# Moving the statistics of x1's third chunk from VectorE to ScalarE in a fused mix, group-norm and convolution-scan kernel

## The reference

```python
x = x + mix(_gn(x), centers, spreads, token_bias)      # a 128x128 map over the positions, one for each of 4 heads
x = x + scan(_gn(x), W)                                # carry = row + relu(conv1d(carry, W)), row after row

def _gn(v, G=32, eps=1e-05):
    g = v.reshape(B_, H_, W_, G, C_ // G)
    m = jnp.mean(g, axis=(1, 2, 4), keepdims=True)
    s = jnp.var(g, axis=(1, 2, 4), keepdims=True)
    return ((g - m) / jnp.sqrt(s + eps)).reshape(v.shape)
```

## Time and profile before

| | before |
|---|---|
| median of three runs | 765.4 us (765.18 to 765.99) |
| profiled execution: its own time | 766.88 us |
| profiled execution: span | 765.1 us |
| PE busy | 681.2 us (89%) |
| DVE busy | 595.5 us (78%) |
| ACT busy | 490.2 us (64%) |
| POOL busy | 429.6 us (56%) |
| granted TensorE clock, mean | 0.973 |

### The profile page before, as it was taken

How to read it: one execution, slowest core, us unless ns; L and a number is a source line. 1 busy time by engine, 2 the same in 40 slices (tenths; PEclk the granted TensorE clock), 3 DMA queues, 4 the chain that set the end, 5 groups by cost and what they waited for, 6 DMA issues and landing times.

```text
span 765.1 us, 18263 instructions
## 1 busy us (share of the span) xinstructions
PE 681.2 (89%) x5100; PEld 648.2 (85%) x5100; DVE 595.5 (78%) x1426; ACT 490.2 (64%) x854; POOL 429.6 (56%) x416
## 2 busy tenths in 40 slices
PE   1578777776999999999899999996999999999995
PEld 1466666666999999999799999986999999999995
DVE  7578999983898888896979898774667677767774
ACT  1156777776676777766676768746666666666661
POOL 1555555661666766665576767752655555555554
PEclk9888999997999999999999999997999999999998
DMA  9855565322355555554555543331444444444444
GB/s 185 160 111 111 117 132 118 75 63 49 71 106 107 103 100 97 106 102 82 101 108 103 108 82 56 56 53 25 78 71 72 76 72 69 72 75 73 69 75 77
DMA packets 412050, 68.18 MB, mean 89 GB/s; under 512 B 411988, under 2 KB 411988, under 8 KB 411988
## 3 DMA queue, kind: packets, MB, share of 16 engines
q1 hardware_dynamic: 359764, 61.17, 43.8%
q10 hardware_dynamic: 52224, 6.30, 5.3%
HBM read 33.85 MB, written 33.55 MB: 88 GB/s over the span
## 4 chain that ended last, share of the span: by engine, by line
PE 45%; DVE 18%; issue 14%; SPq 8%; ACTq 7%; ACT 6%; DMA 1%; POOL 1%; DVEq 0%; POOLq 0%
PE ps_conv L994 21%; PE ps_conv L998 10%; PE ps_mix L918 8%; SPq L299 7%; ACTq L503 6%; DVE st L605 5%; PE ps_in L931 4%; DVE carry L791 3%; ACT carry_h L513 2%; DVE st L706 2%; DVE x_sb L699 2%; ACT x_paired L469 2%; ACT rows L491 2%; PE ps_small L908 2%; DVE carry_l L801 1%
## 5 line engine op out<-in xcount | busy, mean ns | idle before, releaser
L388 POOL TENSOR_TENSOR total<-x_paired,carry 128x256 f32<-128x256 f32 x256 | 250.1, 977 | 226.7 <-DVE staged L778 220.1
L513 ACT ACTIVATE carry_h<-carry 128x256 fp32r<-128x256 f32 x252 | 105.3, 418 | 176.0 <-DVE carry L791 127.6
L491 ACT ACTIVATE rows<-x_paired,shift,rstd 128x256 f32 (+1 forms) x256 | 213.5, 843 | 0.2
L994 PE MATMUL ps_conv<-carry_h,wh 128*128 128x256 f32 x1280 | 205.8, 291 | 6.2 <-ACT carry_h L513 5.7
L998 PE MATMUL ps_conv<-carry_l,wh 128*128 128x256 f32 x1280 | 194.4, 282 | 1.1 <-DVE carry_l L801 1.1
L994 PE MATMUL ps_conv<-carry_h,wl 128*128 128x256 f32 x1280 | 194.8, 283 | 0.0
L469 ACT ACTIVATE x_paired<-ps_in,shift 64x512 f32<-64x512 f32 (+1 forms) x256 | 175.0, 684 | 30.7 <-PE ps_in L931 26.6
L801 DVE TENSOR_TENSOR carry_l<-carry,carry_h 128x256 fp32r<-128x256 f32 x252 | 138.1, 548 | 55.9 <-ACT carry_h L513 40.0
L994 PEld LDWEIGHTS ps_conv<-carry_h,wh 128*128 128x128 f32 x1280 | 172.1, 191 | 11.2 <-ACT carry_h L513 9.1
L998 PEld LDWEIGHTS ps_conv<-carry_l,wh 128*128 128x128 f32 x1280 | 170.9, 190 | 1.5 <-DVE carry_l L801 1.3
L994 PEld LDWEIGHTS ps_conv<-carry_h,wl 128*128 128x128 f32 x1280 | 172.0, 190 | 0.0
(11 more groups left out here) (89 smaller groups left out, 290.5 us busy)
## 6 DMA issues: line engine op xcount, KB each, us to landing
x_sb<-in_x_dram SPq DMA_DIRECT2D x52, 512.0 KB, 4.1
out_dram<-staged SPq DMA_DIRECT2D x832, 32.0 KB, 1.6
rows<-in_x_dram SPq DMA_DIRECT2D x12, 512.0 KB, 4.0
out_dram<-staged ACTq DMA_DIRECT2D x192, 32.0 KB, 1.8
x_paired<-in_L_conv_W_dram SPq DMA_DIRECT2D x2, 80.0 KB, 2.7
x_paired<-in_L_conv_W_dram SPq DMA_DIRECT2D x2, 64.0 KB, 2.6
x_paired<-v_attention_centers_dram SPq DMA_DIRECT2D x1, 0.0 KB
x_paired<-v_attention_spreads_dram SPq DMA_DIRECT2D x1, 0.0 KB
```

The source lines that it names most:

```text
L388: nc.gpsimd.tensor_tensor(total[s][:, :].rearrange("p (w j) -> p w j", w=WS), x1_rows(wave, it, i, 1, s * WS, WS)[:, 0, :, :], carry[s][:, ...
L491: nc.scalar.activation(rows[:, g % 2, :, w // WS, :, w % WS], x1_rows(wave, it, g * RG, RG, w, 1)[:, :, 0, :], ACT.Identity, scale=rstd2[: ...
L513: nc.scalar.activation(carry_h[s][:, EDGE:EDGE + J, :].rearrange("p j w -> p (j w)"), carry[s][:, :], ACT.Copy).then_inc(high_ready[s], 1)
L994: nc.tensor.matmul(ps_conv[:, s * BANK:s * BANK + SW], w[:, d, :], carry_h[s][:, d:d + J, :].rearrange("p j w -> p (j w)"), start=(w is wh ...
```

## The change

ACT takes over the statistics of the third chunk (number 2) of batches 0 to 6. While it keeps this chunk, each of its four ACTIVATEs also sums what it writes (`accum_out`) into `sums2`. After it has kept chunk 3 of the same batch, and ahead of `dev2_of` of the next, a new function `squares2` runs on ACT: a Copy of 128 x 2 scales the sums to means, then two ACTIVATEs of 128 x 512 square the difference of x1 and the mean and sum it; their element output goes to `staged`, which nothing reads in this stage. Means and sums of squares are written into `st2` in the form that `bn_stats` gives, and the counts there are filled in once at the start. On DVE the two `bn_stats` of this chunk go, for the seven batches, and `moments2` waits for the squares (`squares2_done`) and combines seven results where it combined eight. The keeping of chunk 2 of the next batch waits until the squares have read the sums. Batch 7 and the other stages are as before.

```diff
@@ setup
+        sums2 = sb("sums2", [P, 2])
+        mean_c_ready = sem("mean_c_ready")
+        squares2_done = sem("squares2_done")
@@ ScalarE
-            def keep_in(b, k, wave, bw, c, first, count, free):
+            def keep_in(b, k, wave, bw, c, first, count, free, sums=None):
...
                     ins = nc.scalar.activation(dst[q * C:(q + 1) * C, r:CR:2, :], src[:, q, :, :],
-                                               ACT.Identity, bias=shift1[r * C:(r + 1) * C, k:k + 1])
+                                               ACT.Identity, bias=shift1[r * C:(r + 1) * C, k:k + 1],
+                                               accum_out=None if sums is None else sums[q * C:(q + 1) * C, r:r + 1])
...
+            def squares2(b):
+
+                slot = (TU - 1) * (b % 2)
+                act.wait_ge(in_kept, b * CH + CH - 1)
+                if b > 1:
+                    act.wait_ge(mv_ready, b - 1)
+                nc.scalar.activation(st2[:, slot, 1:6:3], sums2[:, :], ACT.Copy,
+                                     scale=1.0 / (HR * J)).then_inc(mean_c_ready, 1)
+                act.wait_ge(mean_c_ready, b + 1)
+                for r in range(2):
+                    nc.scalar.activation(staged[:, r, :], x1_chunk(0, b, CH - 2)[:, r:CR:2, :],
+                                         ACT.Square, scale=-1.0, bias=st2[:, slot, 1 + 3 * r:2 + 3 * r],
+                                         accum_out=st2[:, slot, 2 + 3 * r:3 + 3 * r]).then_inc(squares2_done, 1)
@@ ScalarE, first stage
                     keep_in(b - 1, (b - 1) % 2, 0, b - 1, CH - 1, 0, 4, None)
+                    squares2(b - 1)
                 dev2_of(b + 1)
...
-                keep_in(b, b % 2, 0, b, 2, 0, 4, None)
+                if b > 0:
+                    act.wait_ge(squares2_done, 2 * b)
+                keep_in(b, b % 2, 0, b, 2, 0, 4, None, sums2 if b < W - 1 else None)
@@ VectorE
+            nc.vector.memset(st2[:, 0:TU:TU - 1, 0:6:3], HR * J)
...
+            def shares(b):
+
+                return isinstance(b, int) and b < W - 1
+
             def stats2(b, wave, bw, c, u):
...
-                nc.vector.bn_stats(st2[:, 2 * c + u, :], x1_unit(wave, bw, c, u)).then_inc(stats2_done, 1)
+                slot = 2 * c + u
+                if shares(b):
+                    slot = 2 * min(c, CH - 2) + u + 1
+                nc.vector.bn_stats(st2[:, slot, :], x1_unit(wave, bw, c, u)).then_inc(stats2_done, 1)

             def moments2(b):
-                seen = held(dve, TU * b + TU)
+                first, last = 0, TU
+                seen = held(dve, TU * b + TU - 2 * (W - 1))
+                if shares(b):
+                    seen = (TU - 2) * (b + 1)
+                    first, last = b % 2, TU - 1 + b % 2
                 alone(dve, consts)
+                if shares(b):
+                    dve.wait_ge(squares2_done, 2 * (b + 1))
                 dve.wait_ge(stats2_done, seen)
-                nc.vector.bn_aggr(mv[:, :], st2[:, :, :].rearrange("p n k -> p (n k)")).then_inc(mv_ready, 1)
+                nc.vector.bn_aggr(mv[:, :], st2[:, first:last, :].rearrange("p n k -> p (n k)")).then_inc(mv_ready, 1)
@@ VectorE, alone_chunk, c == 0
                     stats1(nb, ne, 9, 4)
-                    if b > 0:
-                        stats2(b - 1, 0, b - 1, 2, 0)
-                        stats2(b - 1, 0, b - 1, 2, 1)
                     stats1(nb, ne, 13, 3)
```

## The result

The changed kernel takes 768.2 us as the median of 11 runs (765.84 to 771.04), where the kernel before takes 764.6 beside it (11 runs, 762.92 to 767.38). The ratio is 1.0055, with a 95% interval of 1.0031 to 1.0078: **4.2 us slower**, 2.4 to 6.0 (the two medians are 3.6 apart). The forecast was 766.2 us and "within 0.2%"; the measured time lies in the range, but it moved clearly, and the likeliest case was the wrong one. The profiled execution of the changed kernel took 770.53 us (span 768.7).

What follows compares the result with a forecast made beforehand. ACT's chain of keeps and gaps was taken as the bound, DVE setting only the gap before the next batch's chunk 0. -1.26 - 0.5 + 2.4 + 0.2 = +0.84 us gave a median of 766.2 us, range 763.0 to 768.8.

Steps and rivals of the forecast that it cites:

- the likeliest case: Whole kernel: a time within 0.2% of the kernel before, given a chance of 0.42.
- The saving in the early batches: ACT's gaps before chunk 0 after batches 0 and 1 shrink by 0.69 and 0.32 us; earlier clock gives -0.5.
- The sums while keeping: ACT's four summing keeps of chunk 2 cost 0.48 us a chunk: +2.4 in batches 2 to 6, +0.2 in 0 and 1.
- What bounds the kernel: First stage: DVE sets only ACT's gap from chunk 3 to next chunk 0; its relief brings at most 0.65 us a batch.
- rival 3: First stage: DVE is the bound in earnest, its 9.0 us come back in full, 756.4 us; chance 0.04.
- The parts on DVE: DVE drops 1.28 us a batch, `dev_of` stops being late; `moments2` waits nothing for squares, with over 1 us cover.
- `squares2` in the fourth gap: ACT's gap from chunk 3 to next chunk 0, with Copy and two 0.71 us squares: 1.93 us against 1.98.
- the three terms: Batches 0 and 1: shorter ACT gaps (0.69 and 0.32 saved), early clock -0.5, sums while keeping +0.2 us.
- Rival 2: ACT's sums in chunk 2: accumulator reads not hidden, 0.79 us longer a batch, 768.1 us; chance 0.20.
- its decision point: Unhidden reads on ACT: from 0.62 us a chunk on, the time is over 1.5 us longer.
- Rival 1: ACT's sums in chunk 2: accumulator reads fully overlapped, chunk costs 0.05 us more, 763.9 us; chance 0.30.
- rival 4: ACT's squares: their reads not hidden either, 7 x 0.42 = 2.9 us on top of unhidden keep reads, 771.0 us; chance 0.04.

Runs made afterwards that it cites:

- e12: The kernel before, unedited, run again for its profile alone: 763.35 us, first stage 134.01 us.
- e10: The kernel before, unedited, run again for its profile alone: 765.15 us, first stage 136.34 us.
- e4: Against the kernel before, DVE's two `bn_stats` of chunk 2 left out for seven batches, nothing done on ACT instead: 760.9 us, ratio 0.9930.
- e11: The changed kernel, unedited, run again for its profile alone: 768.95 us, first stage 138.80 us.
- e2: The changed kernel without the sums in ACT's four keeps of chunk 2; Copy, squares and DVE's relief stay: 764.7 us, ratio 0.9987 to the kernel before.
- e7: The changed kernel with only the two keeps summing whose source and destination are the same 64 partitions: 768.2 us in one run, period 17.18 us.
- e8: The changed kernel with only the two keeps summing that cross from one half of the partitions to the other: 768.7 us in one run, period 17.40 us.

## Why the prediction was wrong, point by point

Two terms of the sum failed. The saving in the early batches (-1.01 for two long gaps and -0.5 for the clock) was read from one execution with a low clock; e12 has neither gap and e10 only the first. The sums while keeping were put at 0.48 us a chunk and measured 0.61, and in the profiles with the higher clock they are on the path in seven batches, not five.

**What bounds the kernel** held. DVE sets only the fourth gap, the turning holds it at 1.33, and e4 shows it: 1.28 us of DVE's work gone, 0.65 us of period won. The forecast of rival 3, 9 us, is excluded: the interval of e4 ends at 7.5.

**The parts on DVE** held. `dev_of` is done 1.4 us before ACT wants it, and the new wait of `moments2`, 0.41 us, delays nothing: DVE still waits 0.76 us for PE after it. It is less cover than the 1 us and more of the prediction, but cover.

**`squares2` in the fourth gap** held to 0.01 us: 1.92 against 1.93. The Exp of the setup was the right row: the square is 0.71 to 0.73 long and the next begins 0.72 behind it, at the trace's resolution.

**The sums while keeping** were mis-sized, 0.61 and not 0.48. I had the start of a read waited for and its end hidden. It is the other way round for the straight keeps (start hidden, end not), and for the crossing ones neither is hidden. The Trainium skill's rule that ACTIVATEs back to back overlap by 93 ns ("ScalarE: Activation LUTs", What ACT_TABLE_LOAD costs) fits the squares and their reads (91.42 + 0.19 is 91.61, the next square begins at 91.52), if a read is counted as one of them. It doesn't fit what follows a keep: the next keep begins 0.01 us after the end of the one before, and so does the read behind a crossing keep. It doesn't fit a keep behind a read either (84.54 + 0.20 to 84.75). The step also failed where it took the sums of batches 0 and 1 as covered by PE: from chunk 2 to chunk 3 it takes 4.71 and 4.70 there in e11 and 4.10 and 4.09 in e12, so they are on the path in full.

**The early batches** are the larger of the two steps that failed. Against the profile that I had, the saving came and was even larger: the two early gaps are 1.93 after, and batches 0 and 1 together took 36.2 us for 38.4, 2.2 less where the three terms (-1.01, -0.5, +0.2) give 1.3 less. That whole first stage is 1.26 longer, not far from the +0.84 of the forecast, which is in part luck, since each steady batch cost 0.13 us more than forecast (0.56 for 0.43) and two of them had further delays of 0.28 and 0.41. But those gaps were long because PE ran at the lower clock for part of that stretch, and the same kernel also runs without them: one profile's delay was taken for the kernel's own. Without this saving, and with 0.2 for batches 0 and 1 put at two full chunks, my own sum is 7 x 0.48 - 7 x 0.05 = +3.0, over the 1.5 us that can be told; with the measured 0.61 and the gap of batch 0 (+0.50) it is 4.5.

**The rivals.** Rival 2 had the right side and size (768.1 us forecast) for half the right reason: the reads are hidden in half of their places, and its decision point, 0.62 us a chunk, held only with the early saving booked: the measured 0.61 lies under it, and the kernel is slower all the same. Rival 1 is excluded by the period and by the time; rival 4 by the squares, whose reads are overlapped.

**What stays open.** All four profiles of the changed kernel have one period of 17.86 to 17.88 at the same place, batch 4, where chunk 3's turning comes 0.27 late; no other kernel has it, and its cause wasn't tested. Three of them also have 18.0 in batch 6, beside a stretch at 1.2 GHz at 150 us, which e11 doesn't have. What sets the granted clock in the early batches isn't shown: no run sets it, and both values of 34 to 57 us came with both kernels. Nor is it shown whether the change itself spares the low stretch of 57 to 75 us, which two of four profiles of the kernel before have and none of four of the changed one; e2, e7 and e8 have 0.91 there.

## What to carry to other kernels

Work that is moved off a busy engine is worth only what the next limit leaves (here 0.65 us of 1.28 a batch), so move just that much, and put it where the other engine already waits: a separate pass of 0.7 us in a gap was free, while four sums folded into instructions on the path cost 0.61. Before a saving is booked in a stretch with a low granted clock, profile a second execution. An accumulator that is read is an instruction of its own, and its price depends on what stands before and behind it.

## What was not expected of the hardware

- The start of an accumulator read (0.18 to 0.20 us) was hidden behind the keeps that write the partitions that they read, and not behind those that cross from one half to the other (or: behind the first and fourth of a row, and not the second and third); its end was hidden by 0.09 us ahead of a square or `dev2_of`, and not ahead of a keep from `ps_in`. A straight sum added 0.09 us to the chain and a crossing one 0.21 (e7, e8).
- The same program took 134.0 to 138.7 us for the same stage in four profiles, with a mean granted clock in 34 to 57 us of 0.93 in the shortest and of 0.78 to 0.79 in the other three. In e10 (136.3) only batch 0 was slow, and batch 1 took 17.03 with a clock of 1.00 in 57 to 75 us, where the two slowest had 0.81.
